# Attention block with seven-product projections: the output projection's products, its weights' split and three engines' shares are rearranged

## The chip, the cores and the metric

The kernel runs on one NeuronCore of one Trainium2 chip, in a single launch. The time is device microseconds, the median of the runs shown. All data are float32; products are made from pairs of rounded halves (see below), so that they keep float32 accuracy on TensorE.

## What is computed

```
xn  = layernorm(x)                                   # x: 4 x 512 tokens x 1024
qkv = xn @ w_qkv                                     # 32 query heads, 8 key/value heads, 128 each
scores = q k^T * 128**-0.5 - slope[h] * sqrt(i - j)  # causal: j > i is left out
attn   = softmax(scores) @ v                         # per batch and head
att    = attn (4 x 512 x 4096) @ w_o (4096 x 1024)
ffn    = xn @ W^T + b + routed low-rank term (rank 8, 16, 32 or 64 by a gate)
out    = x + att + ffn
```

## The kernel before

Every float32 operand is split in two: ACT writes the rounded "high" (helper `high`, L741), DVE subtracts it and writes the "low" (helper `low`, L944), and PE makes three matmuls per product (L500 to L502: high x high, high x low, low x high). All engines run hand-written orders with semaphores; every engine carries out its own stream in order, so a wait holds up all that stands behind it on that engine.

**Projections.** The batches go in two pairs (`pr`). For each pair seven weight matrices of 1024 x 1024 are taken in turn: VALUES, KEYS, FFN, Q0 to Q3. Each is multiplied by seven block products (Strassen-Winograd) in place of eight; one block product is a *step* of 48 matmuls, 16 products of 512 columns. A step `n` uses eight PSUM banks in halves of four, and its weights come in two halves through three buffers `w_hi`, `w_lo`: ACT and DVE split half 0 of step n+1 at the start of step n, once PE has ended step n-1, and half 1 in its middle. Between the two stands `leave(n - 1)`, which empties the banks of the step before. In steps 1, 4, 5 (emptied in 2, 5, 6) DVE adds the banks to a block, ACT writes its high (`res_hi`, 128x2048), DVE its low, and POOL stores each as 1 MB to DRAM (`qk_s`, L418; `v_s`, L414). At step 0 DVE also makes three sums of raw weight blocks, at step 1 a fourth. SP loads the raw weights (1 MB blocks) when the low of a step is done.

```
before = 2 * n + half - 3          # act.weights(n, half), n the step to come
if before % 2: act.wait_ge(s_bank, 4 * (before // 2 + 1))
else:          act.wait_ge(s_first, before // 2 + 1)
```

**Attention.** 128 *units* (batch, head) in sets of four heads that share keys and values. In an iteration PE computes the scores of unit n, the ten 128x128 transposes of the probabilities of unit n-1 (L687), the output projection of an earlier set (`fill_in`: two of the eight (token tile, column half) blocks of the set, 12 products each, 24 matmuls an iteration), and the product with v of unit n-1 (`attend`). DVE takes the row extremes (L1181), inverts the row sums, scales the probabilities (L1195), makes lows, and adds each finished fill to the running result `acc` (L1214). ACT makes exponentials (L881) and highs. The output weights `w_o` are loaded and split in each of the first pair's and second pair's eight groups beside the attention (`wo_raw`, `wo_hi`, `wo_lo`, 64 blocks of 128x1024). POOL only loads `acc` and stores results then; q, k and v come over SP's queue, q two units ahead.

Of the kernel before, what the change touches and what calls it, by code (L numbers as in the profile page):

```python
# [7 lines left out]
ALU = mybir.AluOpType  # L8
# [5 lines left out]
P = 128  # L14
# [38 lines left out]

def block_program(nc, x, w_all, w_o, w_ag, w_lora, gate_b, consts, out):
    with ExitStack() as ctx:
# [32 lines left out]
        d_lo = at("d_lo", 192 * K + 10624, [P, 512], F32R)  # L88
        rest = 192 * K + 12800
# [20 lines left out]
        wo_raw = at("wo_raw", 24 * K, [P, 2, HIDDEN])  # L110
# [5 lines left out]
        wo_hi = [at(f"wo_hi{i}", (76 + 32 * i) * K, [P, G, HIDDEN], F32R) for i in range(2)]  # L116
        wo_lo = [at(f"wo_lo{i}", (92 + 32 * i) * K, [P, G, HIDDEN], F32R) for i in range(2)]
        at_hi = at("at_hi", 140 * K, [P, 2, G, SEQ], F32R)
        at_lo = at("at_lo", 156 * K, [P, 2, G, SEQ], F32R)
# [5 lines left out]
        lora_s = nc.dram_tensor("lora_s", (2, LK, HIDDEN), F32).ap()  # L125

# [61 lines left out]
        s_wo_raw = [sem(f"s_wo_raw{i}") for i in range(2)]  # L188
        s_wo_hi = sem("s_wo_hi")
        s_wo_lo = sem("s_wo_lo")  # L190
# [10 lines left out]
        s_at_hi = sem("s_at_hi")  # L201
        s_at_lo = sem("s_at_lo")
# [75 lines left out]
        def tiles_of(s):  # L278

            b = unit(s * G)[2]  # L280
            return [(b * QT + t, half) for t in range(QT) for half in range(2)]

        def fills(n):

            s, c = (n - 1) // G - 1, (n - 1) % G
            if s < 0 or s >= SETS:
                return []
            part = tiles_of(s)[2 * c:2 * c + 2]
            return [(s, tt, half, 8 * s + 2 * c + i) for i, (tt, half) in enumerate(part)]

        def chunk_in(n):

            if n < G:
                return n
            if n % (2 * G) < G or n >= UNITS - 2 * G:
                return None
            return (n // (2 * G) + 1) * G + n % G
# [4 lines left out]
        def _(sp):  # L302
# [15 lines left out]

            tokens(0, 0)
# [6 lines left out]
            for pr in range(PAIRS):  # L326
                for m in range(MATRICES):
                    if m == VALUES:
                        sp.wait_ge(s_xt, 2 * TT * (pr + 1))
                        sp.dma_start(ag_raw[:, :], w_ag).then_inc(s_ag_raw, 16)  # L330
                    follow = None if pr == PAIRS - 1 and m == MATRICES - 1 else (m + 1) % MATRICES
# [5 lines left out]
                    sp.dma_start(raw[3][:, :], w_all[m, 3]).then_inc(s_raw[3], 16)  # L337
                    if m == LAST and follow is not None:
                        tokens(pr + 1, 0)
# [13 lines left out]


            sp.wait_ge(s_bank, 4 * (number(PAIRS - 1, LAST, 2) + 1))
            for n in range(UNITS):
# [6 lines left out]
                if n == 2 * HEADS:  # L363
                    sp.wait_ge(s_store_h, stores_h(2, VALUES, 0))
                    sp.wait_ge(s_store_a, stores_r(2, VALUES, 0))
                    sp.wait_ge(s_store_b, stores_r(2, VALUES, 0))
# [10 lines left out]
                c = chunk_in(n)  # L377
                if c is not None:
                    if c == 0:
                        sp.wait_ge(s_bank, 4 * (number(PAIRS - 1, LAST, 3) + 1))  # L380
                    if c >= 2:
                        sp.wait_ge(s_wo_lo, c - 1)
                    head = c % HEADS
                    sp.dma_start(wo_raw[:, c % 2, :], w_o[bass.ds(head * P, P), :]).then_inc(s_wo_raw[c % 2], 16)

        @block.gpsimd
        def _(pool):
# [21 lines left out]
            def store(m, pr, i, j, level, source, signal):  # L409

                b = pr * 2 + j
                if m == VALUES:
                    for t in range(QT):
# [5 lines left out]
                               source).then_inc(signal, 16)  # L419

# [4 lines left out]
            for pr in range(PAIRS):  # L425
                for m in range(MATRICES):
# [32 lines left out]
                    for c, (i, j, res, signal) in enumerate(((0, 0, res_a, s_store_a), (1, 1, res_a, s_store_a),  # L459
                                                             (0, 1, res_b, s_store_b))):  # L460
# [36 lines left out]
        def _(pe):  # L497
# [182 lines left out]
            def transposes(n):  # L680
                pe.wait_ge(s_probs, n + 1)
                for (to, _, _), blocks in zip(t_banks, (
                        [(0, i) for i in range(4)], [(1, 1), (1, 2), (1, 3), (3, 3)], [(2, 2), (2, 3)])):
                    if to is ps_o and n:
                        pe.wait_ge(s_at_lo, n)
# [623 lines left out]
```

## Time and profile before

| | us |
|---|---|
| median of the runs shown (3) | 2569.18 |
| lowest, highest | 2568.89, 2577.41 |
| the profiled execution | 2571.17 |
| its span | 2569.4 |
| PE busy | 2488.9 (97%) |
| DVE busy | 1637.1 (64%) |
| ACT busy | 1025.1 (40%) |
| POOL busy | 176.0 (7%) |
| DMA moved | 355.09 MB, mean 138 GB/s |

The profile is of one execution. "Busy" of PE counts each matmul with its whole passage, and matmuls overlap, so times between starts are shorter than the durations. The idle time in a group's row is that just before its instructions, with the engine that ended it.

### The profile page before, as it was taken

To read this page: it belongs to the slowest core of one execution; us is meant where nothing else is said; L and a number is where in the kernel's file an instruction comes from. 1 tells how busy PE (TensorE), PEld (TensorE's weight loads), DVE (VectorE), ACT (ScalarE), POOL (GpSimd) and SP (SyncE) were. 2 spreads that over 40 slices of the span, in tenths; PEclk is the share of its full clock that TensorE was granted. 3 is DMA by queue.
4 is the path that set the end of the run, shared out by engine and by line. 5 is a ranking of instruction groups with operands and counts; after the bars stand their busy time and mean duration, and the time that the engine had idled before them with its cause. 6 is when DMAs were issued, how large, how long until landed. Compare 5 with 4: busy or idle time off the path is not lost.

```text
span 2569.4 us, 32277 instructions
## 1 busy us (share of the span) xinstructions
PE 2488.9 (97%) x12512; PEld 2124.6 (83%) x12512; DVE 1637.1 (64%) x3305; ACT 1025.1 (40%) x2123; POOL 176.0 (7%) x230
## 2 busy tenths in 40 slices
PE   5999999996999999998899999999999999999998
PEld 4787888885778888887788888888888888888887
DVE  6657445555656455654866777677766777677763
ACT  4432133334533133333544444444444444444441
POOL 3211000001231000001000000000010000000000
PEclk8999999998999999999999999999999999999999
DMA  4536354464355435545632323232353233232311
GB/s 149 181 131 221 115 188 162 174 222 171 103 166 203 148 131 197 187 157 189 224 107 100 105 93 115 92 111 86 131 197 115 90 116 115 83 107 92 122 66 66
DMA packets 86489, 355.09 MB, mean 138 GB/s; under 512 B 8873, under 2 KB 9017, under 8 KB 77376
## 3 DMA queue, kind: packets, MB, share of 16 engines
q1 hardware_dynamic: 49680, 216.65, 24.3%
q0 software_dynamic: 36656, 136.38, 15.1%
q8 instruction: 99, 1.62, 0.3%
q14 instruction: 54, 0.44, 0.1%
HBM read 235.02 MB, written 117.97 MB: 137 GB/s over the span
## 4 chain that ended last, share of the span: by engine, by line
PE 91%; DVE 4%; ACT 2%; issue 1%; POOL 1%; DMA 1%; SPq 0%; DVEq 0%; ACTq 0%; POOLq 0%
PE ps L500 29%; PE ps L502 28%; PE ps L501 28%; PE ps L687 5%; DVE stats L958 1%; ACT rows L770 1%; ACT res_hi L741 1%; DVE w_lo L944 0%; DVE res_a L1034 0%; DVE res_a L944 0%; DVE res_b L1034 0%; ACT w_hi L741 0%; DVE res_b L944 0%; DMA rows<-x 0%; ACT probs L881 0%
## 5 line engine op out<-in xcount | busy, mean ns | idle before, releaser
L944 DVE TENSOR_TENSOR w_lo<-raw,w_hi 128x1024 fp32r<-128x1024 f32 x196 | 239.3, 1225 | 362.5 <-ACT w_hi L741 362.4
L500 PE MATMUL ps<-x_hi,w_hi 128*128 128x512 f32 x1120 | 436.7, 390 | 0.0
L502 PE MATMUL ps<-x_hi,w_lo 128*128 128x512 f32 x1120 | 436.3, 390 | 0.0
L501 PE MATMUL ps<-x_lo,w_hi 128*128 128x512 f32 x1120 | 436.2, 389 | 0.0
L741 ACT ACTIVATE w_hi<-raw 128x1024 fp32r<-128x1024 f32 x196 | 207.3, 1059 | 565.3 <-PE ps L502 445.1
L500 PE MATMUL ps<-wo_hi,at_hi 128*128 128x512 f32 x1024 | 412.1, 402 | 1.4 <-DVE at_lo L944 1.4
L502 PE MATMUL ps<-wo_hi,at_lo 128*128 128x512 f32 x1024 | 401.0, 392 | 0.0
L501 PE MATMUL ps<-wo_lo,at_hi 128*128 128x512 f32 x1024 | 398.7, 389 | 0.0
L881 ACT ACTIVATE probs<-probs,neg_max 128x512 f32<-128x512 f32 (+3 forms) x512 | 283.7, 565 | 193.9 <-DVE neg_max L1181 193.9
L1214 DVE TENSOR_TENSOR acc<-ps,acc 128x512 f32<-128x512 f32 x256 | 176.7, 690 | 164.1 <-issue 135.3
L741 ACT ACTIVATE at_hi<-ps 128x512 fp32r<-128x512 f32 x128 | 76.7, 599 | 509.2 <-PE ps L502 509.2
L502 PEld LDWEIGHTS ps<-x_hi,w_lo 128*128 128x128 f32 x1120 | 210.3, 188 | 43.7
L501 PEld LDWEIGHTS ps<-x_lo,w_hi 128*128 128x128 f32 x1120 | 210.4, 188 | 43.6
L500 PEld LDWEIGHTS ps<-x_hi,w_hi 128*128 128x128 f32 x1120 | 210.4, 188 | 43.0
L502 PEld LDWEIGHTS ps<-wo_hi,at_lo 128*128 128x128 f32 x1024 | 192.3, 188 | 42.6
L501 PEld LDWEIGHTS ps<-wo_lo,at_hi 128*128 128x128 f32 x1024 | 193.1, 189 | 37.0
L500 PEld LDWEIGHTS ps<-wo_hi,at_hi 128*128 128x128 f32 x1024 | 192.6, 188 | 36.9 <-DVE at_lo L944 1.6
L944 DVE TENSOR_TENSOR pt_lo<-ps,pt_hi 128x512 fp32r<-128x512 f32 (+1 forms) x384 | 207.1, 595 | 22.8 <-ACT pt_hi L741 22.8
L1181 DVE CUSTOM_DVE_ANT_0 probs<-ps,bias 128x512 f32<-128x512 f32 (+3 forms) x512 | 219.6, 485 | 0.4 <-PE ps L502 0.4
L944 DVE TENSOR_TENSOR at_lo<-ps,at_hi 128x512 fp32r<-128x512 f32 x128 | 88.4, 691 | 177.9 <-ACT at_hi L741 177.9
L500 PE MATMUL ps<-w_hi,x_hi 128*128 128x512 f32 x448 | 178.2, 398 | 5.3 <-DVE w_lo L944 2.9
L501 PE MATMUL ps<-w_lo,x_hi 128*128 128x512 f32 x448 | 176.8, 395 | 0.0
(147 smaller groups left out, 4051.7 us busy)
## 6 DMA issues: line engine op xcount, KB each, us to landing
raw<-w_all SPq DMA_DIRECT2D x70, 1024.0 KB, 5.3
q<-qk_s SPq DMA_DIRECT2D x128, 512.0 KB, 3.8
qk_s<-res_hi POOLq DMA_DIRECT2D x40, 1024.0 KB, 4.6
wo_raw<-w_o SPq DMA_DIRECT2D x64, 512.0 KB, 4.5
qk_s<-res_a POOLq DMA_DIRECT2D x20, 1024.0 KB, 9.1
qk_s<-res_b POOLq DMA_DIRECT2D x20, 1024.0 KB, 5.3
k<-qk_s SPq DMA_DIRECT2D x32, 512.0 KB, 3.6
v<-v_s SPq DMA_DIRECT2D x32, 512.0 KB, 5.7
```

The lines of the kernel that those rows point to most:

```text
L500: pe.matmul(to, st_hi, mv_hi, start=start, stop=False, skip_group_check=True)
L501: pe.matmul(to, st_hi, mv_lo, start=False, stop=False, skip_group_check=True)
L502: return pe.matmul(to, st_lo, mv_hi, start=False, stop=stop, skip_group_check=True)
L687: last = pe.transpose(to[:, c * P:(c + 1) * P], probs[:, n % 2, OFF[i] + j * P:OFF[i] + (j + 1) * P], ident[:, :])
L741: nc.scalar.activation(to, source, ACT.Copy).then_inc(signal, 1)
L770: nc.scalar.activation(tile, tile, ACT.Identity, bias=shift[:, 2 * t + j:2 * t + j + 1], scale=rstd[:, 2 * t + j:2 * t + j + 1]).then_inc( ...
L881: nc.scalar.activation(tile, tile, ACT.Exp, bias=neg_max[:, i:i + 1], scale=-1.0, accum_out=row_sum[:, i:i + 1]).then_inc(s_exp, 1)
L944: nc.vector.tensor_tensor(to, source, high.bitcast(F32), ALU.subtract).then_inc(signal, 1)
L958: last = nc.vector.bn_stats(stats[:, j, half, :], rows[:, 2 * t + j, half * 512:(half + 1) * 512])
L1181: nc.vector.tensor_tensor_reduce(out=probs[:, n % 2, OFF[i]:OFF[i] + (i + 1) * P], in0=score_bank[i], in1=bias[:, h, SEQ - (i + 1) * P:SEQ ...
L1214: nc.vector.tensor_tensor(to, fill[f % 2][:, :], to, ALU.add).then_inc(s_acc, 1)
```

## The change

- The output projection of a set takes, for each of two token tiles, seven block products (128 tokens x 256 rows x 512 columns, 6 matmuls each) in place of eight; each is a fill of its own that DVE adds to `acc`: 14 fills a set, 4, 3, 4, 3 to an iteration, spread over three places of PE's iteration.
- The seven combinations of `w_o` (16 chunks, 7 splits each) are made once, beside the eight query projections (two splits a step: the first ahead of the next weights' half 1, the second behind it), and stored to DRAM (`wo_s`). In attention they are loaded ready, seven 1 MB blocks a group, on SP's queue; so are `acc` and the results.
- ACT writes the attention output unsplit (`at_raw`); GpSimd makes the combinations (`out_sum`, 8 a set) and the lows (`out_low`, 14 a set), ACT the highs (`out_high`).
- The scaling of the probabilities goes from DVE to ACT (`normalise`).

```diff
+OUT_SUMS = ((0, 3), (1, 3), (0, 2), (0, 6), (0, 4), (1, 2), (1, 6), (1, 4))
+OUT_SPLITS = (0, 1, 6, 3, 4, 2, 5)
+        wp_raw = at("wp_raw", 192 * K, [P, 4, 512])
+        wp_hi = at("wp_hi", 200 * K, [P, 512], F32R)
+        wp_lo = at("wp_lo", 202 * K, [P, 512], F32R)
...
+        def splits(pr, m, st):
+            if m not in QUERIES:
+                return []
+            first = 2 * ((pr * G + QUERIES[m]) * STEPS + st)
+            return [(i // STEPS, i % STEPS) for i in (first, first + 1)]
...
+            def store_splits(pr, m, first, end):
+                for st in range(first, end):
+                    for c, i in splits(pr, m, st):
+                        k, count = OUT_SPLITS[i], STEPS * c + i + 1
+                        mine = slice(c % 2 * 512, c % 2 * 512 + 512)
+                        pool.wait_ge(s_wp_hi, count)
+                        pool.dma_start(wo_s[c // 2, k, :, 0, mine], wp_hi[:, :].bitcast(F32)).then_inc(s_wp_store, 16)
+                        pool.wait_ge(s_wp_lo, count)
+                        pool.dma_start(wo_s[c // 2, k, :, 1, mine], wp_lo[:, :].bitcast(F32)).then_inc(s_wp_store, 16)
...
+                        store_splits(pr, m, (0, 2, 5)[c], (2, 5, 6)[c])
                         pool.wait_ge(s_res_hi, lo + c + 1)
                         store(m, pr, i, j, 0, res_hi[:, :, :].bitcast(F32), s_store_h)
...
+            def out_split(c, i):                       # on ACT
+                k = OUT_SPLITS[i]
+                if c or i:
+                    act.wait_ge(s_wp_store, 32 * (STEPS * c + i))
+                if k in SUM:
+                    act.wait_ge(s_wp_sum, 4 * (c + 1))
+                else:
+                    act.wait_ge(s_wp_raw, 32 * (c + 1))
+                high(wp_hi[:, :], wp_raw[:, WEIGHT[k], :], s_wp_hi)
...
                         gate_ends(pr, m, st)
                         later_operand(pr, m, st, 1)
+                        for part in splits(pr, m, st)[:1]:
+                            out_split(*part)
                         weights(n + 1, 1)
                         gate_parts(pr, m, st)
                         ahead(pr, m, st)
+                        for part in splits(pr, m, st)[1:]:
+                            out_split(*part)
...
+            def out_split(c, i):                       # on DVE
+                dve.wait_ge(s_wp_hi, STEPS * c + i + 1)
+                if c or i:
+                    dve.wait_ge(s_wp_store, 32 * (STEPS * c + i))
+                low(wp_lo[:, :], wp_raw[:, WEIGHT[OUT_SPLITS[i]], :], wp_hi[:, :], s_wp_lo)
+                if i == 2:
+                    dve.wait_ge(s_wp_lo, STEPS * c + i + 1)
+                    out_sums()
...
-                for h in range(G):
-                    last = product(fill[f % 2][:, :],
-                                   (at_hi[:, s % 2, h, t * P:(t + 1) * P], at_lo[:, s % 2, h, t * P:(t + 1) * P]),
-                                   (wo_hi[g % 2][:, h, cols], wo_lo[g % 2][:, h, cols]), h == 0, h == G - 1)
+                for kt in range(2):
+                    cols = slice(kt * 512, (kt + 1) * 512)
+                    last = product(fill[f % 2][:, :], (op_hi[:, part, kt, :], op_lo[:, part, kt, :]),
+                                   (wo[:, k, 0, cols], wo[:, k, 1, cols]), kt == 0 and k in STARTS, kt == 1)
...
+            def normalise(n):                          # on ACT
+                act.wait_ge(s_inv, n + 1)
+                for i in range(QT):
+                    tile = probs[:, n % 2, OFF[i]:OFF[i] + (i + 1) * P]
+                    last = nc.scalar.activation(tile, tile, ACT.Copy, scale=row_inv[:, i:i + 1])
+                last.then_inc(s_probs, 1)
```

Three places in the engines' orders. First ACT, steps 1 (end of its start) to 3 of a query projection; `w_hi` are the highs of the coming step's weights, `res_` those of `leave`. Before:

```order
L741 ACTIVATE w_hi<-raw_57 128x1024 [waits s_sum,s_bank]
L741 ACTIVATE res_hi<-res_a 128x2048 [waits s_drain_v,s_store_h]
L741 ACTIVATE w_hi<-raw_57 128x1024 [waits s_first]
L741 ACTIVATE w_hi<-raw_56 128x1024 [waits s_sum,s_bank]
L741 ACTIVATE res_b<-ps 128x512 [waits s_bank,s_store_b]
L741 ACTIVATE res_b<-ps 128x512 [waits s_bank] x3
L741 ACTIVATE w_hi<-raw_56 128x1024 [waits s_first]
```

After, the same stretch:

```order
L871 ACTIVATE w_hi<-raw_57 128x1024 [waits s_sum,s_bank]
L871 ACTIVATE res_hi<-res_a 128x2048 [waits s_drain_v,s_store_h]
L871 ACTIVATE wp_hi<-wp_raw 128x512 [waits s_wp_sum,s_wp_store]
L871 ACTIVATE w_hi<-raw_57 128x1024 [waits s_first]
L871 ACTIVATE wp_hi<-wp_raw 128x512 [waits s_wp_sum,s_wp_store]
L871 ACTIVATE w_hi<-raw_56 128x1024 [waits s_sum,s_bank]
L871 ACTIVATE res_b<-ps 128x512 [waits s_bank,s_store_b]
L871 ACTIVATE res_b<-ps 128x512 [waits s_bank] x3
L871 ACTIVATE wp_hi<-wp_raw 128x512 [waits s_wp_sum,s_wp_store]
L871 ACTIVATE w_hi<-raw_56 128x1024 [waits s_first]
L871 ACTIVATE wp_hi<-wp_raw 128x512 [waits s_wp_raw,s_wp_store]
```

Two highs of `w_o` combinations (`wp_hi`) stand in each step, one ahead of each following `w_hi`, and all but the first of the kernel wait for `s_wp_store`, the landing of the stores of the split before.

POOL's queue over the same steps, with the stores of the block (`qk_s`) and of the splits (`wo_s`). Before:

```order
L418 DMA qk_s<-res_hi 128x4x512 [waits s_res_hi]
L418 DMA qk_s<-res_a 128x4x512 [waits s_res_lo]
L418 DMA qk_s<-res_hi 128x4x512 [waits s_res_hi]
L418 DMA qk_s<-res_a 128x4x512 [waits s_res_lo]
L418 DMA qk_s<-res_hi 128x4x512 [waits s_res_hi]
```

After:

```order
L519 DMA wo_s<-wp_hi 128x512 [waits s_wp_hi]
L521 DMA wo_s<-wp_lo 128x512 [waits s_wp_lo]
L519 DMA wo_s<-wp_hi 128x512 [waits s_wp_hi]
L521 DMA wo_s<-wp_lo 128x512 [waits s_wp_lo]
L509 DMA qk_s<-res_hi 128x4x512 [waits s_res_hi]
L509 DMA qk_s<-res_a 128x4x512 [waits s_res_lo]
L519 DMA wo_s<-wp_hi 128x512 [waits s_wp_hi]
L521 DMA wo_s<-wp_lo 128x512 [waits s_wp_lo]
L519 DMA wo_s<-wp_hi 128x512 [waits s_wp_hi]
L521 DMA wo_s<-wp_lo 128x512 [waits s_wp_lo]
```

Between the pairs of block stores there are now four or more, up to twelve, stores of splits, and the first of them after a pair stands behind it in the queue.

SP's queue at the start of attention, the loads of units 2 and 3. Before:

```order
L371 DMA q<-qk_s 128x1024 [waits s_scores]
L384 DMA wo_raw<-w_o 128x1024 [waits s_wo_lo]
L371 DMA q<-qk_s 128x1024 [waits s_scores]
L384 DMA wo_raw<-w_o 128x1024 [waits s_wo_lo]
```

After:

```order
L462 DMA q<-qk_s 128x1024 [waits s_scores]
L419 DMA wo<-wo_s 128x2048 [waits s_wp_store,s_bank]
L419 DMA wo<-wo_s 128x2048 x6
L425 DMA acc<-acc_s 128x1024 [waits s_store_b,s_store_a,s_store_h]
L425 DMA acc<-acc_s 128x1024 x7
L462 DMA q<-qk_s 128x1024 [waits s_scores]
L461 DMA k<-qk_s 128x1024 [waits s_scores]
```

The loads of all seven weight blocks and of the eight `acc` tiles stand between the q of unit 2 and the q of unit 3.

## Rows read from the trace of the kernel before

**Rows 1.** The page: engines; then the table of stretches (us, busy us, instructions).
```profile
PE 2488.9 (97%) x12512; PEld 2124.6 (83%) x12512; DVE 1637.1 (64%) x3305; ACT 1025.1 (40%) x2123; POOL 176.0 (7%) x230
...
700.00:1180.00 480.00, 478.28 (x2118) 392.28 (x2117) 265.25 (x265) 157.53 (x185) 50.60 (x68) 1.00 0.50 174
1260.00:2500.00 1240.00, 1240.00 (x6926) 1094.10 (x6925) 881.86 (x2382) 547.74 (x1488) 8.49 (x16) 1.00 0.31 108
```

**Rows 2.** Timeline of one attention unit: start us, us, engine, line, operation, tiles, count.
```profile
1801.43 0.39 PE L500 MATMUL ps<-k,q 128*128 128x512 f32 x1
...
1803.34 1.25 PE L687 MATMUL ps<-ident,probs 128*128 128x128 f32 x10
...
1804.35 0.48 PE L500 MATMUL ps<-wo_hi,at_hi 128*128 128x512 f32 x1
...
1804.92 1.62 DVE L944 TENSOR_TENSOR pt_lo<-ps,pt_hi 128x512 fp32r<-128x512 f32 x3 [0.33 <-ACT pt_hi L741]
...
1809.92 0.39 PE L500 MATMUL ps<-pt_hi,v 128*128 128x512 f32 x1
...
1811.82 0.39 PE L500 MATMUL ps<-k,q 128*128 128x512 f32 x1
```

**Rows 3.** Timeline of the query projections: ACT, then DVE (idle before, and who ended it).
```profile
1004.77 1.92 ACT L741 ACTIVATE res_hi<-res_a 128x2048 fp32r<-128x2048 f32 x1 [3.75 <-DVE res_a L1034]
...
1010.84 1.06 ACT L741 ACTIVATE w_hi<-raw 128x1024 fp32r<-128x1024 f32 x1 [3.21 <-PE ps L502]
...
1021.72 1.06 ACT L741 ACTIVATE w_hi<-raw 128x1024 fp32r<-128x1024 f32 x1 [4.38 <-PE ps L502]
...
985.88 2.29 DVE L1021 TENSOR_TENSOR raw<-raw,raw 128x2048 f32<-128x2048 f32 x1
...
1006.72 2.29 DVE L944 TENSOR_TENSOR res_a<-res_a,res_hi 128x2048 f32<-128x2048 f32 x1 [2.04 <-ACT res_hi L741]
```

**Rows 4.** Groups by line and shape: busy us, mean ns of one, idle before.
```profile
L1214 DVE TENSOR_TENSOR acc<-ps,acc 128x512 f32<-128x512 f32 x256 | 176.7, 690 | 164.1 <-issue 135.3 <-PE ps L502 28.8
...
L944 DVE TENSOR_TENSOR wo_lo<-wo_raw,wo_hi 128x1024 fp32r<-128x1024 f32 x64 | 78.1, 1221 | 24.2 <-ACT wo_hi L741 24.2
...
L741 ACT ACTIVATE wo_hi<-wo_raw 128x1024 fp32r<-128x1024 f32 x64 | 67.6, 1056 | 43.0 <-PE ps L502 43.0
...
L1195 DVE TENSOR_SCALAR probs<-probs,row_inv 128x512 f32<-128x512 f32 x128 | 61.6, 481 | 0.0
...
L741 ACT ACTIVATE res_a<-ps 128x512 f32<-128x512 f32 x96 | 49.0, 595 | 3.7 <-DMA v_s<-res_a 3.7
L741 ACT ACTIVATE pt_hi<-ps 128x256 fp32r<-128x256 f32 x128 | 48.5, 379 | 0.3 <-PE ps L687 0.3
...
L770 ACT ACTIVATE rows<-rows,shift,rstd 128x1024 f32<-128x1024 f32 x16 | 19.0, 1234 | 7.1 <-DVE shift L977 7.1
...
L399 POOL TENSOR_TENSOR x_raw<-x_raw 128x512 f32<-128x512 f32 x8 | 10.3, 1282 | 36.8 <-DVE x_raw L985 22.4 <-ACT x_raw L741 14.3
```

**Rows 5.** DMA issues of single moments (138.5, 976.7, 1009.3 and 1010.2 us) and the q loads: KB, us to landing.
```profile
v_s<-res_hi POOLq DMA_DIRECT2D x1, 256.0 KB, 2.8
...
qk_s<-res_b POOLq DMA_DIRECT2D x1, 1024.0 KB, 5.2
...
qk_s<-res_a POOLq DMA_DIRECT2D x1, 1024.0 KB, 10.0
raw<-w_all SPq DMA_DIRECT2D x1, 1024.0 KB, 8.0
...
q<-qk_s SPq DMA_DIRECT2D x128, 512.0 KB, 3.8
```

**Rows 6.** Start of attention: PE's timeline, then the DMA of 1217 to 1240 us.
```profile
1218.06 0.77 PE L500 MATMUL ps<-k,q 128*128 128x512 f32 x1 [9.49 <-DVE res_b L944]
...
1235.85 0.63 PE L500 MATMUL ps<-k,q 128*128 128x512 f32 x1
...
DMA packets 2094, 7.81 MB, mean 340 GB/s; under 512 B 190, under 2 KB 190, under 8 KB 2093
```

More of the change, by code:

```diff
@@ L109, in block_program @@
         v = at("v", 16 * K, [P, 2, 2, SEQ], F32R)
-        wo_raw = at("wo_raw", 24 * K, [P, 2, HIDDEN])
+        at_raw = [at(f"at_raw{i}", (24, 42)[i] * K, [P, G, SEQ]) for i in range(2)]
         dist = at("dist", 32 * K, [P, SEQ])
@@ L276, in unit @@
             return pr, g, b, h
-        def tiles_of(s):
-            b = unit(s * G)[2]
-            return [(b * QT + t, half) for t in range(QT) for half in range(2)]
         def fills(n):
@@ L317, in weights, with chunk @@
                 sp.dma_start(raw[i][:, :], w_all[m, i]).then_inc(s_raw[i], 16)
+            def chunk(pr, m, i):
+                c = 2 * (pr * G + QUERIES[m]) + i
+                if m == Q0 and i == 0:
+                    sp.wait_ge(s_bank, 4 * number(pr, FFN, 6) + 4)
+                if c:
+                    sp.wait_ge(s_wp_lo, STEPS * c)
+                for half in range(2):
+                    head = c // 2 * G + 2 * half + c % 2
+                    sp.dma_start(wp_raw[:, half::2, :],
+                                 w_o[bass.ds(head * P, P), :].rearrange("p (j c) -> p j c", j=2)).then_inc(s_wp_raw, 16)
             tokens(0, 0)
@@ L376, in _ @@
                                  v_s[pr * 2 + b, g].rearrange("p l t d -> p l (t d)")).then_inc(s_v[s % 2], 16)
[L377 to L384, printed above, removed]
+                out_weights(n)
+                results(n)
+            for t in range(2 * QT):
+                sp.wait_ge(s_acc, PARTS * (SETS - 2 + t // QT) + (STEPS if t % 2 == 0 else PARTS))
+                store_out(PAIRS - 1, t // QT, t % QT)
+            for tt in range(TT):
+                sp.wait_ge(s_out[tt], 16 * PAIRS)
         @block.gpsimd
@@ L730, in _ @@
                     scores(n)
+                todo = fills(n)
+                for f in todo[:1]:
+                    fill_in(*f)
                 if 1 <= n <= UNITS:
                     transposes(n - 1)
-                for f in fills(n):
+                for f in todo[1:3]:
                     fill_in(*f)
@@ L736, in _ @@
                     attend(n - 1)
+                for f in todo[3:]:
+                    fill_in(*f)
         @block.scalar
@@ L926, in _ @@
                     transposed(n - 1)
-                if n < UNITS:
-                    for c in range(1, QT):
-                        if n:
-                            exponential(n, c)
-                    if chunk_in(n) is not None:
-                        out_weights(chunk_in(n))
+                if 1 <= n < UNITS:
+                    for c in range(1, QT):
+                        exponential(n, c)
+                for part in later:
+                    out_high(*part)
+                if n < UNITS:
+                    normalise(n)
         @block.vector
@@ L1243, in _ @@
                         later_operand(pr, m, st, 1)
+                        for part in splits(pr, m, st)[:1]:
+                            out_split(*part)
                         weights(n + 1, 1)
```

242 lines of the change are left out of this document (161 added, 81 removed).

## The prediction

> **What bounds the kernel now.** I read the page's busy shares first, then a table of stretches, then two timelines. PE is busy for 97% of the span; in 700 to 1180 us (projections) it is busy 478 of 480 us, in 1260 to 2500 (attention) all of 1240, at full clock [rows 1]. So projections and attention are both PE-bound, and time comes off only where PE issues less, as long as nobody else becomes late. "Busy" isn't the price of a matmul: a 512-column one is shown as 0.39 us long, but 24 of the output projection take from 1804.35 to 1809.92, which is 0.232 from start to start [rows 2]. One attention unit (scores, ten transposes, 24 output matmuls, attend) lasts from 1801.43 to 1811.82, 10.39 us. In the projections ACT's first weight high of a step comes at 1010.84 and that of the next at 1021.72: 10.88 us a step (48 matmuls), 76.2 us for the seven of a matrix [rows 3].
>
> **Removed from PE.** A set has 84 output matmuls in place of 96, so over 32 sets 384 go. At 0.232 that is **-89 us**, all of it on the path. The busy column (0.39 each) would have promised 150; it is the wrong column.
>
> **Attention, the others.** DVE loses per unit the low of the output (a 512-column operation, 0.69), half a weight low (1.22/2) and four scalings (the longest 0.48, together about 1.5), and gains 1.5 additions of 0.69 [rows 4]: from 7.4 us (882/1240 x 10.39 [rows 1]) to about 5.6. ACT has 4.6 us; it loses half a weight high (0.53), gains 3.5 highs of 256 columns (0.38 by the PSUM row [rows 4], which I take at 0.40) and the four scalings. A scaling on ACT is not in the trace. From below it is the plain high (512 columns 0.60, 256 columns 0.38), from above the row with a scale and a bias from columns (1024 elements, 1.23 against 1.06 for the plain one), so 0.2 more on each: 1.8 to 2.6 for the four, and I take 2.2, since one column operand is nearer to none than to two plus a table entry. ACT gets to 7.7 of a new period of 9.7. GpSimd gets 22 operations of 256 columns a set; 512 columns take it 1.28 [rows 4], so 0.64 each and up, 14 to 18 us of 39. None of the three binds. The tightest spot: between transposes and attend PE had 24 matmuls, now 12. From the first transpose (1803.34) to the end of the third low it took 3.2 us (1804.92 + 1.62); the new distance is 1.1 + 12 x 0.232 = 3.9. That leaves 0.7. I put 0 on it, and +20 as the upper end.
>
> **Start and end of attention.** The weights come as seven 1 MB loads and the running sums as eight of 0.5 MB, all now on SP's queue in unit 2, ahead of the q of unit 3. Before, the sums went on POOL's queue, and 7.81 MB took the 23 us of that window at 340 GB/s [rows 6]. 11.5 MB at 0.4 MB/us is 29 us, and unit 3's scores started at 1235.85, 18 us after those of unit 1: **+12** (4 to 20). The end has the same tail of additions and one more share of fills: +2 (0 to 4).
>
> **The split of the output weights, moved beside the query projections.** Two splits a step, 14 a matrix, 8 matrices. Their work is small: 0.60 on ACT, 0.69 on DVE (the 512-column rows [rows 4]), two 256 KB stores on POOL. PE's slack would cover that. What matters is that there is one wp_hi and one wp_lo: ACT's high of a split waits until *both* stores of the split before have landed, and it stands in ACT's queue ahead of the high of the next projection weights; DVE's low does the same. I call it the ring. Its gaps, from high to high:
> - plain: 0.60 + 0.69 + 2.8 for a 256 KB store that has the queue to itself [rows 5] + 0.1 = 4.2; five of them, 21.
> - two that also wait for the next w_o block (0.60 + 0.69 + 3.8, the q load's time): 10.
> - two around DVE's three sums of projection weights (3 x 2.28 [rows 3]), before which the second low can't start: 13, an estimate.
> - three in steps 2, 5 and 6, where the first split stands behind the block's addition (four of 0.69, 2.5 with their overlap), its high (1.92 [rows 3]) and a weight low (1.2), after the last split's own 1.3: 6.9 each, and 3 more for the four sums of w_o in one: 24. (The other four sums cost 0.5.)
> - three behind a 2 MB pair of block stores. The block's low (2.29 [rows 3]) ends 2.3 after the split's high, its 1 MB store is issued, and the split's two stores queue behind it. That 1 MB store lands after 5.2 us when SP is quiet, after 10.0 when SP loads 1 MB of weights beside it [rows 5], which it does in steps 2 and 5. With 1.2 for the 0.5 MB of the split: 8.7, and twice 12.5 at most, 11 where the load starts 1.5 to 2 us later, as it will: 31.
>
> Sum 99 us a matrix against PE's 76.2. As soon as the ring is slower than PE, each step's w_lo waits for it: PE's slack is the three weight buffers, about 5 to 9 us, used up in the first matrix. So a group of four query matrices loses about 5 in the first, 3 x 22.8 in the others, and 10 when the lag passes to what follows (the next batch pair's operands, or attention): 83, and two groups **+167**. Bounds: with every block store landing as if alone and quick stores the ring is 90, and two groups lose 98; with each contended gap at 13 and the load gaps at 7 it is 106, and they lose 212. A second cost lies here: PE will idle up to 9 us at a time. At 1218.06, after 9.49 us of idling, a 512-column matmul takes 0.77 where it takes 0.39 to 0.48 elsewhere [rows 2, 6]: it ran at the lower of the two levels, 1.2 GHz. I put nothing on it, because PE has 23 idle us a matrix in which to be slow; its upper end is 20. The Trainium skill ("TensorE: Matmul & The Clock Gate", on the two states) has the clock fall after idling, so by it this upper end is more than a fringe; the rows 6 agree.
>
> **Sum.** -89 + 12 + 2 + 167 = **+92** on the profiled execution's 2571.2 (its span is 2569.4), 2663; the median of the runs shown is 2.0 below that, so **2661 us**.
>
> **Rivals.**
> - *The ring fits (faster).* If the block stores let small ones through, and sums and waits fall into gaps that the ring has anyway, the 14 gaps stay near 5, 70 in all, under 76.2, and only -89 + 12 + 2 is left: 2494. For it: a plain pair of gaps (8.4) is less than a step (10.88). Against it: a block store lands 5 to 10 us after its issue, three times a matrix, in order on one queue. It decides at 76.2 us a matrix. 0.15.
> - *Half way.* The ring is just over PE, 80 to 88 a matrix: losses of 40 to 90 against the 75: 2534 to 2584. 0.15, split over the three outcomes.
> - *Attention doesn't speed up.* The 0.7 us before attend isn't there, or ACT's scalings are at 0.9 each; then a unit keeps its 10.39 and the 89 are not earned: 2750. Against it: ACT at 7.7 of 9.7. 0.08.
> - *The forecast*, ring at 90 to 106: 2580 to 2740. 0.62.
>
> **Range and chances.** 0.5% is about what a measurement can tell from no change (13 us). Slower: 0.62 + 0.08 + 0.04 = 0.74; same (2556 to 2582) 0.07; faster 0.15 + 0.04 = 0.19. The range leaves out the first rival and most of the third: 2560 to 2740.
>
> **What would show it.** In the page after: PE's busy share well under 97%, with the loss inside the query matrices only, 95 to 103 us each where values, keys and FFN keep 76; wp_hi on ACT waiting for the landing of wo_s stores as one of the largest waits, and projection w_lo ending after PE's need; a unit of 9.7 us in attention, with DVE near 58% and ACT near 79%; the first fills 12 us later. Wrong if query matrices take 76 to 80 us (first rival), or if a unit stays above 10.2.

## The result, and the profile after

| | before | after |
|---|---|---|
| median of the runs | 2569.65 us | 2740.36 us (2738.62 to 2744.98) |
| ratio | | 1.066 (95%: 1.0635 to 1.0684) |
| span of the profiled execution | 2569.4 us | 2737.5 us |

The change is slower by 171 us. The forecast was slower by 92 (2661 us, range 2560 to 2740): the side and the mechanism held, the size fell short, and the median lies at the very end of the stated range.

The page after: engines, the chain that ended last, and the issues of the stores of the split output weights (KB each, us to landing).
```profile
PE 2483.8 (91%) x12128; PEld 2089.0 (76%) x12128; DVE 1578.4 (58%) x2969; ACT 1402.1 (51%) x3131; POOL 785.6 (29%) x1126
...
PE 61%; DMA 15%; DVE 12%; ACT 5%; issue 4%; POOL 2%; SPq 1%; DVEq 0%; ACTq 0%; POOLq 0%
...
wo_s<-wp_hi POOLq DMA_DIRECT2D x112, 256.0 KB, 2.9
wo_s<-wp_lo POOLq DMA_DIRECT2D x112, 256.0 KB, 3.8
```
PE went from 97% busy [rows 1] to 91%, and the chain now runs through transfers for 15% of the span. The table of stretches tells where (us, then busy us and instructions of PE, PEld, DVE, ACT, POOL; granted clock, DMA share, GB/s):
```profile
700.00:1180.00 480.00, 423.40 (x1787) 342.67 (x1787) 277.21 (x323) 165.97 (x209) 92.83 (x128) 0.93 0.51 176
...
1520.00:2660.00 1140.00, 1140.00 (x6448) 1002.47 (x6447) 708.93 (x1874) 830.74 (x2291) 460.57 (x642) 1.00 0.48 181
715.40:732.50 17.10, 5.93 (x22) 5.46 (x23) 6.54 (x8) 7.84 (x9) 1.84 (x3) 0.50 0.53 209
1473.10:1493.60 20.50, 3.55 (x12) 3.27 (x13) 1.27 (x4) 0.81 (x2) 0.00 (x0) 0.50 0.94 380
```
In attention PE is still busy all of the time. In the projections it is busy for 423 us of 480, where it was 478 [rows 1], though nobody is near its limit: DVE is at 277, ACT at 166. That is the picture of a wait. The table of waits names it (us in all, times, longest):
```profile
DVE wp_lo L1107 <- ACT wp_hi L871: 320.5, 64, 10.7
ACT wp_hi L871 <- DMA wo_s<-wp_lo: 292.6, 65, 12.7
...
PEld ps L624 <- DVE w_lo L1107: 153.5, 48, 8.2
...
ACT wp_hi L871 <- DMA wp_raw<-w_o: 94.5, 16, 7.6
...
PE ps L624 <- DVE w_lo L1107: 75.5, 30, 4.8
...
PE ps L624 <- DVE res_b L1197: 46.5, 7, 11.4
...
PEld ps L624 <- DMA q<-qk_s: 22.1, 1, 22.1
```
ACT waits 293 us for the landing of wo_s stores and 95 for loads of w_o. PE's weight loads (PEld) wait 154 us for the projection's w_lo and its matmuls 76; these two overlap in time and are not to be added. PE also waits for PSUM banks to be emptied (res_b), work that stands behind the splits in DVE's queue. By its busy time PE is idle for 254 us in all, where it was 81. The waits of ACT and of PE are one path. The chain of waits inside one query matrix shows it (start us, us, what):
```profile
1204.31 2.30 DVE res_a L1107
1206.91 0.76 POOL qk_s L509
1207.67 0.53 POOL wo_s L519
1208.21 9.55 DMA wo_s<-wp_lo
1217.76 0.02 issue
1217.78 0.02 ACT wp_hi L871
1217.80 0.51 issue
1218.32 1.05 ACT w_hi L871
...
1235.12 0.70 DVE wp_lo L1107
1235.84 0.55 SPq L369
1236.43 5.87 DMA wp_raw<-w_o
1242.46 0.47 issue
1242.92 1.05 ACT w_hi L871
```
DVE finishes a block's low; POOL issues its 1 MB store and then a split's two stores, the second of which lands 9.55 us after its issue. Then only can ACT make the next wp_hi, and behind it the w_hi that PE needs.

**Where the time went**, from the starts of PE's matmuls. From the first query matrix on, the matrices took 91.6, 109.4, 106.1, 139.6 and, for the second batch pair, 91.7, 108.9, 104.9, 114.3 us (the last up to the start of the last projection matmul, which comes some 7 us after the first scores before, 9 after). Before they took 76.2 each, except the fourth of the first pair (97.1, with the operands of the next pair in it) and that of the second (77.9). That is 121.0 and 113.3 lost; 3.8 came back elsewhere (about 2 outside the query matrices, about 2 because the first scores now start further ahead of that last matmul), so attention starts at 1431.5 instead of 1201.0: **+230.5**. From there to the end it takes 1306.0 instead of 1368.4: **-62.4**. Sum +168.1, the difference of the spans. Of the -62.4, the first five units cost +24.5 (74.1 against 49.6 us), the steady part gives -81.3 (9.727 us a unit against 10.393) and the tail behind the last scores -5.6.

### The profile page after: what moved, and what is told of

Read it like the earlier page. It is cut to its first block, busy times and chain, and to the rows that moved or that the text cites. A ratio compares the mean times of both kernels' runs of the same rounds, so it can differ in the third digit from the quotient of the medians.

```text
span 2737.5 us, 35262 instructions
## 1 busy us (share of the span) xinstructions
PE 2483.8 (91%) x12128; PEld 2089.0 (76%) x12128; DVE 1578.4 (58%) x2969; ACT 1402.1 (51%) x3131; POOL 785.6 (29%) x1126
## 4 chain that ended last, share of the span: by engine, by line
PE 61%; DMA 15%; DVE 12%; ACT 5%; issue 4%; POOL 2%; SPq 1%; DVEq 0%; ACTq 0%; POOLq 0%
PE ps L624 19%; PE ps L626 19%; PE ps L625 19%; DMA wo_s<-wp_lo 8%; PE ps L811 5%; DMA wp_raw<-w_o 3%; ACT res_hi L871 2%; DVE res_a L1197 2%; DVE res_a L1107 2%; DVE wp_raw L1382 1%; ACT w_hi L871 1%; ACT wp_hi L871 1%; DVE res_b L1197 1%; DVE wp_lo L1107 1%; DVE res_b L1107 1%
## 5 line engine op out<-in xcount | busy, mean ns | idle before, releaser
L1375 DVE TENSOR_TENSOR acc<-ps,acc 128x512 f32<-128x512 f32 x448 | 298.2, 688 | 233.9 <-issue 203.9
L624 PE MATMUL ps<-wo,op_hi 128*128 128x512 f32 x896 | 361.0, 403 | 1.7 <-POOL op_lo L596 1.7
L626 PE MATMUL ps<-wo,op_lo 128*128 128x512 f32 x896 | 351.9, 393 | 0.0
L625 PE MATMUL ps<-wo,op_hi 128*128 128x512 f32 x896 | 351.0, 392 | 0.0
L871 ACT ACTIVATE wp_hi<-wp_raw 128x512 fp32r<-128x512 f32 x112 | 70.4, 628 | 414.3 <-DMA wo_s<-wp_lo 292.6
L1107 DVE TENSOR_TENSOR wp_lo<-wp_raw,wp_hi 128x512 fp32r<-128x512 f32 x112 | 77.2, 689 | 320.5 <-ACT wp_hi L871 320.5
L596 POOL TENSOR_TENSOR op_lo<-op_raw,op_hi 128x256 fp32r<-128x256 f32 x256 | 189.6, 752 | 249.6 <-ACT op_hi L871 249.6
L596 POOL TENSOR_TENSOR op_lo<-at_raw,op_hi 128x256 fp32r<-128x256 f32 x192 | 141.1, 742 | 409.4 <-ACT op_hi L871 402.9
L871 ACT ACTIVATE pt_hi<-ps 128x512 fp32r<-128x512 f32 (+1 forms) x384 | 174.5, 528 | 150.2 <-PE ps L811 150.2
L1025 ACT ACTIVATE probs<-probs,row_inv 128x128 f32<-128x128 f32 (+3 forms) x512 | 245.7, 557 | 2.0 <-DVE row_inv L1356 2.0
L624 PE MATMUL ps<-k,q 128*128 128x512 f32 (+3 forms) x512 | 166.8, 326 | 44.8 <-DMA q<-qk_s 21.9
```

Source lines behind the costliest of these rows:

```text
L596: nc.gpsimd.tensor_tensor(op_lo[:, part], op_source(s, part), op_hi[:, part].bitcast(F32), ALU.subtract).then_inc(s_op_lo, 1)
L624: pe.matmul(to, st_hi, mv_hi, start=start, stop=False, skip_group_check=True)
L625: pe.matmul(to, st_hi, mv_lo, start=False, stop=False, skip_group_check=True)
L626: return pe.matmul(to, st_lo, mv_hi, start=False, stop=stop, skip_group_check=True)
L871: nc.scalar.activation(to, source, ACT.Copy).then_inc(signal, 1)
L1025: last = nc.scalar.activation(tile, tile, ACT.Copy, scale=row_inv[:, i:i + 1])
```

## The experiments

All times are compared with the kernel before in the same jobs (2569.5 to 2569.9). Experiments 1 to 7 and 9 are one execution each, 8, 10, 11 and 12 the median of four or five; waits, matrices and units are read from the one that was profiled. "Matrices" are the times between PE's first matmuls of query matrices one to three of the second pair, after 91.7, 108.9, 104.9.

**1. The stores don't read the split.** The stores of the splits read an unrelated tile, and nobody waits for them.
```diff
-                    act.wait_ge(s_wp_store, 32 * (STEPS * c + i))
+                    act.wait_ge(s_wp_lo, STEPS * c + i)
...
-  pool.dma_start(wo_s[c // 2, k, :, 0, mine], wp_hi[:, :].bitcast(F32))
+  pool.dma_start(wo_s[c // 2, k, :, 0, mine], x_hi[:, 6, 3, :].bitcast(F32))
```


> The changed kernel with one edit: the 224 stores of the output weights' splits read a tile that nobody writes at that time (so the stored weights, and with them the result, are not the reference's), and ACT and DVE no longer wait for those stores to land. Same highs, lows, sums, stores and bytes. Ring theory (the wait for the landing, in order ahead of the projection weights, costs the 235 us by which the projections became longer): query matrices fall from 92 to 109 us back to 77 to 82, scores of unit 0 start near 1225 instead of 1431, total 2740 - 200 = about 2535 (2515 to 2560). Rival, traffic (the added 66 MB slow the weight loads and block stores): query matrices stay above 95, total above 2680. Rival, work (two more highs and lows a step on ACT and DVE are too many): the same, above 2680.

Measured: 2575.2 us; matrices 76.2, 84.3, 84.5. All highs, lows, stores and loads are still there; the wait for landings alone was worth 165 us. But 15 us more are left than the ring theory allowed, and two of the matrices are over its 82. The high-to-high gaps of wp_hi say where: 12.1 to 13.0 us at each load of w_o, twice a matrix.

**2. The traffic alone.** Stores and loads as in 1, but no highs, lows or sums of the splits.

> The changed kernel without the highs, lows and sums of the output weights (left out; the stores read another tile, so the result is not the reference's), but with all 224 stores and 32 loads, paced by the projections' own weight lows. If the ring theory holds, neither work nor traffic matters much: query matrices 76 to 78 us, total within 15 us of free_source. If the work on DVE is what remains (step 0 has three sums of 2.3 us and two lows more), it is 10 to 40 us faster than free_source. Traffic theory: still above 2680.

Measured: 2505.9 us; matrices 76.2, 76.2, 76.2. The same stretch of the query projections in this kernel and in that of experiment 1:
```profile
1000.00:1140.00 140.00, 140.00 (x619) 115.95 (x618) 71.94 (x67) 51.90 (x60) 38.26 (x65) 1.00 0.83 306
```
```profile
1000.00:1140.00 140.00, 130.08 (x551) 105.54 (x551) 96.40 (x101) 57.70 (x76) 34.88 (x59) 0.96 0.71 263
```
PE is busy all 140 us while 306 GB/s move. So the transfers cost PE nothing by themselves in this stretch. The matrices came as the ring theory had them, but the time did not: it is 69 us under experiment 1, where the ring theory allowed 15 and its rival, that DVE's work remains, 10 to 40. Something other than the landings still held experiment 1.

**3. The load of w_o in halves.** Experiment 1, with each 512 KB load cut in two with a semaphore each, the first issued one split earlier.
```diff
-                if c:
-                    sp.wait_ge(s_wp_lo, STEPS * c)
                 for half in range(2):
+                    if c:
+                        sp.wait_ge(s_wp_lo, STEPS * c - 1 + half)
```


> As the kernel whose wo_s stores read an unrelated tile (2575 us, so the highs and lows of the splits wait for no store; 64 us were left against the query matrices of before), and with each load of w_o into wp_raw cut in two 256 KB loads with a semaphore each, the first issued one split earlier. The stored blocks are again not those of w_o, so the output is not the reference's. Theory A: what was left is the single wp_raw, whose next load can only start when the last low of a step of seven has read it (those gaps of wp_hi took 12.3 to 13.0 us, two in each matrix, against 5 to 6 of the others). Then each such gap falls by some 4 us, 16 gaps, up to 64: 2510 to 2550. Theory B: what was left is the work itself on DVE and ACT (14 highs, 14 lows and 8 sums a matrix beside the splits of the query weights): 2565 to 2585, and the gaps behind the loads are made up by others.

Measured: 2539.2 us; matrices 76.2, 77.2, 79.3; the gaps at the loads fell to 8.1 to 11.3. The time lies in theory A's range. With 1 and 2 the loss against 2505.9 divides as 165 (landings of stores), 36 (the earlier loads of w_o), and 33 for what is left: the highs, lows and sums and the waits for w_o that remain (ACT's fell from 134.2 to 101.5 us only). 19 of the 33 lie in the last matrix of the two groups (110.9 and 84.6 against 98.8 and 77.9). How the 33 divide between work and waits was not tried apart.

**4. One store of two on SP's queue.** The first split of each step is stored from SP's queue, the second from POOL's, the buffers stay single.

> The changed kernel, result whole: the first split of each step is stored from SP's queue, ahead of that step's weight load; the second stays on POOL's. All waits stay. Ring theory with the queue as its largest part: the gaps of 12.2, 12.6 and 9.4 us (behind the 2 MB block stores) fall to 4 to 6, about 18 us of the ring's 107 a matrix; the ring comes to about 89, query matrices to 84 to 92, total about 2740 - 2 x (3 x 18 + 15) = 2600 (2570 to 2640). If the order in POOL's queue doesn't matter (only that the split stores share the DMA engines with the block stores), it stays above 2710.

Measured: 2657.8 us; matrices 82.2, 94.2, 95.4. 82.5 us come back, 58 fewer than hoped and 18 short of the stated range; 73 of them lie ahead of attention, 9 in its first units. The three gaps behind block stores fell from 12 to 14, 12 to 14 and 9.4 us to 5.7 to 7.8, but the one after the first of them rose from 4.1 to 5.9 up to 7.3 to 8.9, and the ring still took 94 to 97 us in each of the steady matrices.

**5. Experiments 3 and 4 together, with waits for the stores.**

> The first split of each step is stored from SP's queue (alone 2657.8 us) and the loads of w_o are cut in two with the first one split earlier; the result is the reference's. Ring theory: the two w_o gaps of a matrix go from 8 to 5 us, so from 95 to 89 us a matrix, six to eight matrices: 2605 to 2635. Rival, that the matrices of that kernel are bound by DVE and ACT work and not by the ring: 2650 to 2665.

Measured: 2642.9 us; matrices 81.1, 91.8, 95.1. Only 15 us for the halves; the time lies between the two ranges, 8 us above the ring theory's and 7 below the rival's. "ACT wp_hi <- DMA wp_raw<-w_o" fell from 88.9 to 45.7 us, and "ACT wp_hi <- DMA wo_s<-wp_lo" rose from 208.3 to 236.0: the ring took over most of what the loads gave.

**6. The start of attention.** On the changed kernel, the loads of the first seven weight blocks and the running sums go over units 2 to 5.
```diff
-                    for i in range(STEPS):
+                if 2 <= n < 6:
+                    for i in ((0, 1), (2, 3), (4, 5, 6), ())[n - 2]:
                         sp.dma_start(wo[:, i].bitcast(F32), wo_s[0, i]).then_inc(s_wo[i], 16)
-                    for tt in range(TT):
+                    for tt in ((0, 2), (1, 3), (), (4, 6, 5, 7))[n - 2]:
```


> The changed kernel, result whole: the first weight blocks and running sums are loaded over units 2 to 5 instead of all in unit 2, so q of unit 3 has 3 MB ahead of it instead of 11.5. Theory (that queue costs the 22 us wait for q): the first five units take 74 us now, 52 to 58 after, total 2740 - 18 = 2722 (2716 to 2730). If HBM bandwidth at the start of attention is the bound and the order doesn't matter: within 5 us of 2740.

Measured: 2725.3 us. Units 0 to 5 took 21.0, 9.0, 9.7, 10.1, 10.0, 13.5 instead of 21.0, 8.7, 28.9, 8.6, 6.9, 10.5: the one wait of 22.1 us for the q of unit 3 is gone, 11 us of it for good (84.5 against 73.4 for the six units). The other 4 of the 15 us lie ahead of attention, where this edit changes nothing. In experiments 8 and 10 the same edit took 12 us off these units.

**7. and 8. Two buffers.** Pieces of 256 columns, four a step; high and low side by side, one 256 KB store for both, two pairs of buffers; wp_raw twice; half the stores on SP.
```diff
-        wp_raw = at("wp_raw", 192 * K, [P, 4, 512])
-        wp_hi = at("wp_hi", 200 * K, [P, 512], F32R)
-        wp_lo = at("wp_lo", 202 * K, [P, 512], F32R)
+        wp_raw = at("wp_raw", 192 * K, [P, 2, 4, 256])
+        wp = at("wp", 200 * K, [P, 2, 2, 256], F32R)
...
-                    act.wait_ge(s_wp_store, 32 * (STEPS * c + i))
+                    act.wait_ge(s_wp_store[(n - 2) % 4], 16 * ((n - 2) // 4 + 1))
```


> The splits of w_o in pieces of 256 columns, four a step, with high and low side by side in one of two buffers and one 256 KB store of both, two of a step from SP's queue and two from POOL's; two wp_raw, so that the next load runs beside the splits. A high waits only for the store two splits before. The result is the reference's. Ring theory: with two in flight a split of 256 columns has two gaps' time, 2 x 2.7 us of PE's 76.2 for 28 splits = 5.4 us against some 5 of high, low and store, so the query matrices come back to 76 to 84 us each: 2505 to 2570. Rival, that DVE's work (twice as many lows and sums, each half as long, plus what each instruction costs by itself) or the order within the engines' queues holds the matrices at 90 us and more: 2600 to 2680. Rival, that stores on SP hold the loads of the query weights behind them: matrices over 90 us with gaps at raw, not at wp.

> As the one before, with the loads of the blocks of wo and of acc spread over units 2 to 5 instead of all at unit 2 (alone this saved 15 us on the changed kernel, 2740.4 to 2725.3). The result is the reference's. Ring theory: 15 us less than the one before, 2490 to 2555, so faster than the kernel before (2569.6). Rivals: as the one before, less 15 us: 2585 to 2665; or the spread saves nothing here because the query matrices' end is now earlier and the loads of unit 2 meet nothing: same as the one before.

Measured: 2687.4 us and 2673.5 us (ratio 1.0405, 1.0388 to 1.0423); matrices 87.1, 101.4, 98.9. The ring theory's ranges ended over 100 us lower; the times lie 7 and 8 us above the first rival's. Experiment 4, which has one buffer and also half the stores on SP, is 30 us faster than 7. The waits of the second kernel don't show DVE's work, the first reason that this rival gave:
```profile
ACT wp L900 <- DMA wo_s<-wp: 301.4, 110, 8.2
...
ACT wp L900 <- DMA wp_raw<-w_o: 7.6, 2, 3.8
```
Loads are no longer waited for, stores as much as ever. The reckoning of 2.7 us a piece took two buffers for two independent rings. They are not: each engine makes two pieces in a row, both stores mostly leave within 2 us of each other and land, by the median 1.3 us apart, 2.4 to 8 us later, so a pair of small pieces behaves like one large split.

**9. and 10. Four buffers.** The same 12 KB divided otherwise: wp as four buffers, wp_raw once, loaded in halves.
```diff
-        wp_raw = at("wp_raw", 192 * K, [P, 2, 4, 256])
-        wp = at("wp", 200 * K, [P, 2, 2, 256], F32R)
+        wp_raw = at("wp_raw", 192 * K, [P, 4, 256])
+        wp = at("wp", 196 * K, [P, 4, 2, 256], F32R)
```


> As the kernel of 256-column pieces (2687.4 us, in which two pieces are stored side by side and the next two wait till both have landed, 4 to 8 us: still the ring), but with four buffers for high and low, and a single wp_raw whose two halves are loaded apart; the result is the reference's. A high now waits for the store four splits before, so two pairs are in flight. Ring theory: a pair's round of some 7 us then stands for half a step's share of 10.9, and nothing waits for landings: query matrices 76 to 82 us, the time near that of the kernel that stores an unrelated tile and loads w_o in halves (2539.2): 2535 to 2575. Rival, that the landings are slow because all stores and loads together ask for more than the queues carry (then deeper buffers only make the landings longer): matrices stay over 92 us, 2630 to 2690. Rival, that twice the instructions on DVE and ACT hold the matrices: 84 to 90 us, 2575 to 2630, with few waits of wp for a store.

> As the one before, with the loads of wo and acc spread over units 2 to 5 (which saved 15.1 and 13.8 us on two kernels); the result is the reference's. Ring theory: 2520 to 2560, faster than the kernel before (2569.5) by 10 to 50 us. Under the two rivals 2615 to 2675, or 2560 to 2615.

Measured: 2658.5 us and 2643.7 us (ratio 1.0285, 1.0271 to 1.0299); matrices 84.9, 95.5, 95.0. The ring theory's ranges were missed by over 80 us. The times are those that the first rival expected, but not for its reason: its slow landings don't hold the highs. The group of wp's highs in the kernel of 9 (busy us, mean ns | idle before):
```profile
L899 ACT ACTIVATE wp<-wp_raw 128x256 fp32r<-128x256 f32 x224 | 86.6, 412 | 338.0 <-DMA wp_raw<-w_o 198.2 <-DVE wp_raw L1412 127.4 <-DMA wo_s<-wp 12.4
```
The landings are out of the path (12 us). In their place stand the loads, eight of 256 KB a matrix now, and the sums on DVE.

**11. An order that frees blocks early.** On 10: the splits of a chunk go 1, 6, 0, 3, 5, 4, 2, so that blocks 1 and 3 are free two splits before the end, and the next two splits need only these; their loads stand earlier in SP's queue; a high of a sum waits for its own sum.
```diff
-OUT_SPLITS = (0, 1, 6, 3, 4, 2, 5)
+OUT_SPLITS = (1, 6, 0, 3, 5, 4, 2)
+READY = {3: 1, 4: 2, 2: 3, 5: 4}
...
-                    act.wait_ge(s_wp_sum, 4 * (c + 1))
+                    act.wait_ge(s_wp_sum, 4 * c + READY[k])
```


> As the kernel with four buffers of 256 columns and the spread loads (2643.7 us), but the seven splits of a chunk in the order 1, 6, 0, 3, 5, 4, 2, so that blocks 1 and 3 of wp_raw are free two splits before the end of a chunk and the next two splits need only these; and ACT's high of a sum waits for its own sum, not for all four. The result is the reference's. In the kernel with four buffers highs no longer waited for stores; they waited 198 us for loads of w_o (53 times, mean 3.7) and 127 us for the sums on DVE (24, mean 5.3). Theory A: these waits took the place of the ring, and hold up the splits of the query weights behind them on ACT. With two splits' time (5 us) ahead the load waits fall to a third and the sums' by half, so the query matrices come from 95 to 82 to 88 us: 2545 to 2600. Theory B: what holds the matrices is now the amount of work of ACT and DVE in pieces (twice as many instructions), or the transfers themselves: 2625 to 2645, with other waits in the place of these.

Measured: 2580.0 us (ratio 1.0037, 1.0023 to 1.0051); matrices 76.2, 87.7, 86.9. The time and the matrices are theory A's: 64 us from an order and a count, with not an instruction fewer. Its waits fell less than it had: for loads from 196.1 to 133.7 us (it had a third), for sums from 127.4 to 96.8 (half), and waits for stores rose from 12.0 to 36.8. What the order and what the count gave was not tried apart.

**12. One split further.** Blocks 0 and 2 loaded apart (order 1, 6, 0, 3, 5, 2, 4), the loads of the start over units 2 to 9.

> As the kernel before (2580.0 us), with block 0 and block 2 of wp_raw loaded apart (order 1, 6, 0, 3, 5, 2, 4, so block 0 is free one split earlier and block 2 is needed by DVE's sums alone), and with the loads of wo and acc spread over units 2 to 9 instead of 2 to 5. The result is the reference's. In the kernel before highs still waited 133.7 us for loads of w_o and matrices took 86 to 89 us; the first six units took 63.7 us. Theory A (the wait for the next load is what is left): the waits fall to 70 to 100 us, the matrices to 80 to 86 us, 10 to 30 us in all, and the units' start another 3 to 5: 2545 to 2570, level with the kernel before the change (2569.6) or faster. Theory B (the sums of DVE and the number of instructions are what is left): only the start's 3 to 5 us: 2573 to 2578.

Measured: **2559.8 us** (ratio 0.9963, 0.9950 to 0.9977), 10 us under the kernel before; matrices 76.2, 84.2, 83.6; units 0 to 5 take 11.0, 7.0, 8.3, 9.4, 7.0, 10.5. The same group in this kernel:
```profile
L908 ACT ACTIVATE wp<-wp_raw 128x256 fp32r<-128x256 f32 x224 | 86.6, 413 | 216.4 <-DVE wp_raw L1419 100.9 <-DMA wp_raw<-w_o 83.2 <-DMA wo_s<-wp 32.1
```
The wait for loads is 83 us where it was 134 in 11 and 198 in 9. This is the one version with the reference's result that is faster than the kernel before, by less than half a per cent. How its 20 us against 11 divide was read off, not tried apart: attention starts 13.8 us earlier (1279.1 against 1292.9), and units 0 to 5 are 10.5 us shorter (53.2 against 63.7; 3 to 5 were expected). These sum to 24 because the profiled executions are 24 us apart.

## Why the prediction was right and where it was short

- **-89 for the matmuls: right, 4 us too large.** A steady unit takes 9.727 us, forecast 9.7; 128 times the 0.666 us saved is 85, of which 81 lie in the steady part. The wrong column would have said 150.
- **Nobody else late in attention: right.** DVE is busy 709 of 1140 us and ACT 831 (forecast 5.6 and 7.7 of 9.7; read 6.0 and 7.1). The groups by shape (busy us, mean ns):
```profile
L596 POOL TENSOR_TENSOR op_lo<-op_raw,op_hi 128x256 fp32r<-128x256 f32 x256 | 189.6, 752 | 249.6 <-ACT op_hi L871 249.6
...
L1025 ACT ACTIVATE probs<-probs,row_inv 128x512 f32<-128x512 f32 x128 | 91.7, 716 | 0.0
L1025 ACT ACTIVATE probs<-probs,row_inv 128x384 f32<-128x384 f32 x128 | 78.0, 610 | 0.0
...
L1025 ACT ACTIVATE probs<-probs,row_inv 128x256 f32<-128x256 f32 x128 | 64.3, 502 | 0.0
...
L1025 ACT ACTIVATE probs<-probs,row_inv 128x128 f32<-128x128 f32 x128 | 51.0, 399 | 2.0 <-DVE row_inv L1356 2.0
```
  The four scalings take 0.716 + 0.610 + 0.502 + 0.399 = 2.2 us, as taken. GpSimd's half-width low takes 0.75, not 0.64: halving the columns doesn't halve its time. The room before attend, 0.7 us in the forecast, is 0.95 in the steady units; the third rival is out.
- **+12 for the start: right cause, half the size, and outside its 4 to 20.** It was 24.5: 4.0 between units 0 and 1 (21.0 against 17.0), which the forecast hadn't seen, and 19.8 between units 1 and 3 (37.6 against 17.8). PE's first scores of units 0, 1 and 3:
```profile
1431.49 0.77 PE L624 MATMUL ps<-k,q 128*128 128x512 f32 x1 [11.42 <-DVE res_b L1197]
...
1452.50 0.77 PE L624 MATMUL ps<-k,q 128*128 128x512 f32 x1 [11.52 <-DVE res_b L1107]
...
1490.05 0.79 PE L624 MATMUL ps<-k,q 128*128 128x512 f32 x1 [21.86 <-DMA q<-qk_s]
```
  and SP's issues meanwhile:
```profile
1452.54 4.85 SPq L419 DMA_DIRECT2D wo<-wo_s  x7
1467.69 6.16 SPq L425 DMA_DIRECT2D acc<-acc_s  x8
1473.89 1.82 SPq L462 DMA_DIRECT2D q<-qk_s  x1
```
  The weight loads leave at 1452.54, with unit 1's scores, when the last split's store has landed; the sums stand behind the last block's store till 1467.69; the q of unit 3 is issued at 1473.89 and lands with the rest, at 380 GB/s. The forecast took 29 us for the 11.5 MB at 0.4 MB/us; they took 37.5, with the last 2 MB of block stores among them, and at the 340 GB/s of [rows 6] 11.5 MB alone are 34. Experiment 6 shows that it was what stands ahead of that q, not the total that is loaded.
- **+2 for the end: wrong sign, small.** It was -5.6. Its cause stays open.
- **+167 for the ring: right mechanism (experiment 1), too small.** Measured +230.5, 64 of the 76 us by which the terms fell short of the spans' +168. Two things in this step were mis-sized. First the sum of gaps: 99 was forecast, 106.3, 109.4 and 106.3 us came in the first three matrices. The 99 is itself of fifteen gaps (5 + 2 + 2 + 3 + 3), where a matrix has fourteen splits: four gaps are plain, not five, so what was priced is 95. Three gaps of the third matrix of the second pair, from ACT's timeline (the starts are 12.2, 4.1 and 7.8 us apart: behind a block store, plain, with a load):
```profile
1268.00 0.64 ACT L871 ACTIVATE wp_hi<-wp_raw 128x512 fp32r<-128x512 f32 x1 [0.33 <-DMA wo_s<-wp_lo]
...
1280.15 0.63 ACT L871 ACTIVATE wp_hi<-wp_raw 128x512 fp32r<-128x512 f32 x1 [10.57 <-DMA wo_s<-wp_lo]
...
1284.25 0.63 ACT L871 ACTIVATE wp_hi<-wp_raw 128x512 fp32r<-128x512 f32 x1 [0.58 <-DMA wo_s<-wp_lo]
...
1292.04 0.63 ACT L871 ACTIVATE wp_hi<-wp_raw 128x512 fp32r<-128x512 f32 x1 [6.22 <-DMA wp_raw<-w_o]
```
  Plain gaps (4.1 to 5.9, forecast 4.2), the two at DVE's three sums (13 together), sums of w_o and additions (9.9, 7.2) came nearly as forecast. The two with a load of w_o took 7.8 to 9.1 in place of 5: a 512 KB load lands after 5.5 us by its median, there are two of them, one issued behind the other, and they start only after the last low. Those behind block stores took 12.0 to 14.2 twice and 9.4 to 9.5 in place of 11 and 8.7. The forecast's own terms for such a gap beside a load (2.3 + 10.0 + 1.2) are 13.5; it wrote 12.5 at most and took 11 because the load would start later. In all +7 to +10 a matrix over the 99. Second, the slack: the forecast credited PE with 5 to 9 us of weight buffers per group and asked 5 us of the first matrix. It lost 15.4. Four matrices lost 121.0, about 4 x (107 - 76.2) = 123: the lead is spent at once and owed again at the end of the group, so it should have been left out. Of the 64 us, the gaps are some 8 x 7 and the slack the rest, an estimate.
- **The clock.** The forecast put nothing on PE's slower stretches. They came: 0.50 from 715.4 to 732.5, where PE did 5.9 us of work in 17.1, and 0.95 as the mean of the span. The Trainium skill ("TensorE: Matmul & The Clock Gate", on the two states) has the clock fall after idling; the rows agree. In the query matrices PE's time is the ring's: 109.4 and 106.1 us in the second and third, where the fourteen gaps sum to 109.4 and 106.3, at a granted clock of 0.89 and 0.87. There the slower stretches fell into idle time, as the forecast assumed. Outside them it was not tried apart (0.95 after, 0.98 in experiments 3 and 12).
- **The first rival (2494)** was the ring that fits. Experiment 2, which has the transfers but neither the splits' work nor their waits, gives 2505.9, with 24.8 us from unit 2 to unit 3. The nearest kernel with the splits' work in it is experiment 3, at 2539.2.
- **The signs.** The query matrices were to take 95 to 103 us; they took 92 to 109. The other matrices were to keep 76; they kept what they had, which is 80 for keys and 88 for FFN.

## What to carry to other kernels

Cheap work that goes beside a busy engine is priced by its buffers, not by its instructions: write down the ring (make, store, landing, make again), take the landing at the queue's worst neighbour, and set the sum against the time that the covering engine gives; any excess is paid in full. When a ring is too slow, count what each buffer really waits for: here halves of a buffer in pairs gave nothing, the other queue for every second split gave 82 us, and 64 came from an order of use that frees the buffer of the next load two uses earlier, together with waits for single sums. And a wait that is taken away uncovers the next one (landings, then loads, then sums), so read the waits again after each step.

## What the runs showed that was not expected

- 306 GB/s of loads and stores go beside a PE that is busy 140 us of 140 (experiment 2), 263 GB/s with waits beside 130 of 140 (experiment 1).
- Two stores of 256 KB issued 0.6 us apart on one queue land within 0.7 us of each other: in experiment 7 those of 1084.08 and 1084.69 take 7.7 us each, beside a block's 1 MB store on POOL's queue, those of 1140.61 and 1141.16 take 2.5 and 3.2. Moving one split in two to another queue took the gaps behind a 1 MB store beside a load from 12 to 14 us down to 6 to 8 (experiment 4). The Trainium skill ("DMA: Bandwidth & Descriptors", "Queues, rings and completion order") has each DMA engine take turns between the queues it has work for; experiment 4 fits that.
- A 256 KB store takes 2.3 to 2.9 us where nothing is ahead of it, 5.5 at 1228.96, behind a block's store, and 9.55 at 1208.21, behind a block's store and beside a 1 MB load of SP's. The Trainium skill ("DMA: Bandwidth & Descriptors", "Anatomy of one DMA") has 2.0 us plus the bytes over 436 GB/s, by which an estimate is 2.6. The trace agrees with it for the first case; for a ring it is the others that count.
- A single instruction more on ACT's queue can be nearly free or cost 10 us, depending only on which landing it waits for: wp_hi is 0.63 or 0.64 us in the rows of ACT's timeline above, the idle time before it 0.33 to 10.57.
